# Three moves in a two-layer fp32 kernel: the copies of half 0's y, the next batch's first input products, and the next layer's weight remainders

## The reference

```
x = x + attention(norm(x))        # 16 heads of 128, causal with a position bias
x = x + ternary_ffn(norm(x))      # weights quantized by groups of 64, silu(gate)*up, rms norm
x = x + mamba(norm(x))            # below
x = x + sparse_ffn(norm(x))       # silu(gate)*up, 2 of 4 neighbours kept, down product
```

```
x, z = split(in_proj(h))                      # "input products": 512 channels each
x = silu(causal_conv4(x))
dt_low, B_n, C_n = split(x_proj(x))
delta = softplus(dt_proj(dt_low) + bias)
h_n[t] = exp(delta*A_n)[t] * h_n[t-1] + (delta*B_n*x)[t]     # the scan, over t = 0..1023
y[t] = sum_n h_n[t]*C_n[t] + D*x[t]
out = out_proj(y * silu(z))
```

## Time and profile before

| | us |
|---|---|
| median of 3 runs | 1705.2 |
| the profiled execution | 1710.48 |
| its span, as the profile shows it | 1708.7 |
| PE / DVE / ACT / POOL busy | 1608.9 / 1366.3 / 1231.1 / 789.7 |
| mean granted TensorE clock over the span | 0.982 of full speed |

### The profile page before, as it was taken

How to read it: one execution, slowest core, us unless ns; L and a number is a source line. 1 busy time by engine, 2 the same in 40 slices (tenths; PEclk the granted TensorE clock), 3 DMA queues, 4 the chain that set the end, 5 groups by cost and what they waited for, 6 DMA issues and landing times.

```text
span 1708.7 us, 32910 instructions
## 1 busy us (share of the span) xinstructions
PE 1608.9 (94%) x10396; PEld 1437.8 (84%) x10396; DVE 1366.3 (80%) x2301; ACT 1231.1 (72%) x2307; POOL 789.7 (46%) x753
## 2 busy tenths in 40 slices
PE   8999999999999999999998899878889888889998
PEld 7899889988998899889987788678877687877888
DVE  7788878887887788778876667689985789896997
ACT  5777777777777777777776555599995699994443
POOL 4444444444444444444443111359983199891000
PEclk9999999999999999999999999989999999999999
DMA  3100000000000000000000100013220033240000
GB/s 100 32 20 19 25 31 18 18 25 31 16 16 26 28 16 15 25 28 15 15 7 1 52 0 0 2 72 112 99 100 12 2 112 110 87 158 2 7 19 26
DMA packets 25080, 64.11 MB, mean 38 GB/s; under 512 B 2832, under 2 KB 8976, under 8 KB 24752
## 3 DMA queue, kind: packets, MB, share of 16 engines
q1 hardware_dynamic: 25008, 63.17, 11.0%
HBM read 60.94 MB, written 2.23 MB: 37 GB/s over the span
## 4 chain that ended last, share of the span: by engine, by line
PE 65%; POOL 17%; DVE 8%; issue 6%; ACT 2%; DMA 1%; POOLq 0%; DVEq 0%; SPq 0%; ACTq 0%
POOL m_h L2588 15%; PE ps L579 11%; PE ps L541 11%; PE ps L564 7%; PE ps L496 7%; PE ps L592 5%; PE ps L519 5%; PE ps L814 4%; PE ps L721 4%; PE ps L826 2%; PE ps L742 2%; POOL prob L2452 1%; POOL prob L2445 1%; PE ps L1082 1%; PE ps L506 1%
## 5 line engine op out<-in xcount | busy, mean ns | idle before, releaser
L2452 POOL TENSOR_SCALAR prob<-prob,rinv 128x128 f32<-128x128 f32 (+7 forms) x256 | 228.4, 899 | 212.1 <-DVE rinv L1770 205.7
L2445 POOL TENSOR_SCALAR prob<-prob 128x128 f32<-128x128 f32 (+7 forms) x256 | 188.2, 735 | 288.4 <-ACT prob L1186 279.9
L2588 POOL TENSOR_TENSOR m_h<-m_h,m_C 128x1024 f32<-128x1024 f32 x128 | 300.0, 2375 | 42.2 <-DVE m_h L2353 41.7
L2353 DVE TENSOR_TENSOR_SCAN m_h<-m_y,ps 128x1024 f32<-128x1024 f32 x128 | 287.1, 2276 | 30.6 <-PE ps L970 18.3
L1736 DVE TENSOR_TENSOR pt_lo<-ps,pt_hi 128x512 fp32r<-128x512 f32 (+2 forms) x320 | 189.5, 604 | 81.6 <-ACT pt_hi L1199 79.8
L1729 DVE CUSTOM_DVE_ANT_0 prob<-prob,bias 128x128 f32<-128x128 f32 (+7 forms) x256 | 213.9, 853 | 7.8 <-POOL prob L2445 4.7
L1186 ACT ACTIVATE prob<-ps 128x128 f32<-128x128 f32 (+7 forms) x256 | 165.7, 652 | 68.7 <-PE ps L541 68.1
L1199 ACT ACTIVATE pt_hi<-ps 128x512 fp32r<-128x512 f32 (+2 forms) x320 | 163.0, 531 | 65.9 <-PE ps L564 63.8
L1192 ACT ACTIVATE prob<-prob,nmax 128x128 f32<-128x128 f32 (+7 forms) x256 | 198.1, 776 | 3.0 <-DVE nmax L1729 2.0
L1573 ACT ACTIVATE m_u<-m_uT,m_bT 128x256 f32<-128x256 f32 x448 | 185.6, 504 | 0.1
L978 PE MATMUL ps<-ident,m_h 128*128 128x128 f32 x1024 | 140.4, 281 | 36.8 <-POOL m_h L2588 34.7
(11 more groups left out here) (271 smaller groups left out, 4064.6 us busy)
## 6 DMA issues: line engine op xcount, KB each, us to landing
m_C<-bc_dram SPq DMA_DIRECT2D x64, 512.0 KB, 3.6
wqk_raw<-wqk_in SPq DMA_DIRECT2D x16, 512.0 KB, 3.5
wv_raw<-wv_in SPq DMA_DIRECT2D x16, 256.0 KB, 2.6
wo_raw<-wo_in SPq DMA_DIRECT2D x16, 256.0 KB, 2.8
q_raw<-wgu_in SPq DMA_DIRECT2D x8, 256.0 KB, 2.7
raw<-wgu_in SPq DMA_DIRECT2D x1, 2048.0 KB, 8.3
out<-x SPq DMA_DIRECT2D x8, 256.0 KB, 2.1
x<-x_in SPq DMA_DIRECT2D x2, 512.0 KB, 4.5
```

What stands on the lines that cost most here:

```text
L2353: nc.vector.tensor_tensor_scan(m_h[:, 2 * (v % 2) + e, :], m_da[:, 2 * (v % 2) + e, :], drive(e), 0.0, ALU.mult, ALU.add).then_inc(scan_do ...
L2445: nc.gpsimd.tensor_scalar(prob[:, at:at + n], prob[:, at:at + n], CLIP, -CLIP, ALU.min, ALU.max).then_inc(s_clipped, 1)
L2452: nc.gpsimd.tensor_scalar(prob[:, at:at + n], prob[:, at:at + n], rinv[:, k:k + 1], 1.0, ALU.mult, ALU.mult).then_inc(norm_done, 1)
L2588: nc.gpsimd.tensor_tensor(state, state, m_C[:, v, :], ALU.mult).then_inc(hc_done, 1)
```

## The change

Four places. In the order of the diff: PE's `expand` of unit 12 goes behind `add_state` of unit 9 and `add_x` 8 and 9; the first two input products of the next batch go into the end of the scan, one ahead of each of the two last `add_state` (they wait for the scan of unit 30, which frees banks 4 and 5), with ACT copying them from there as before; ACT's copies of y are split, two behind each decay (units 12 and 13); DVE makes weight remainders 1 and 2 ahead of `dve_sparse_rows_lo`.

```
@@ pe_mamba_scan
             pe.wait_ge(scan_done, unit(b, 1, *at(12)) + 3)
             pe_y_turn(pe, b, 0)
-            expand(1, *at(12), after_y=True)
             add_state(1, *at(9))
             add_x(1, 8)
             add_x(1, 9)
+            expand(1, *at(12), after_y=True)
             pe.wait_ge(scan_done, unit(b, 1, *at(13)) + 3)
             pe_y_turn(pe, b, 1)
             add_state(1, *at(10))
...
             for e in range(2):
+                if b < B - 1:
+                    pe.wait_ge(scan_done, unit(b, 1, last, RING - 1, 0) + 5)
+                    pe_in_x(pe, b + 1, (e,))
                 add_state(1, last, RING - 1, e, end=True)
@@ block.tensor
             pe_mamba_scan(pe, 0)
-            pe.wait_ge(scan_done, 4 + 2 * HALF_UNITS)
-            pe_in_x(pe, 1, range(2))
             pe.wait_ge(yz_done, 3)
             pe_mamba_out(pe, 0, (0, 1), range(4))
@@ act_mamba_scan
-            def decays(half, it, v):
+            def decays(half, it, v, y0=False):
                 for e in range(2):
                     act.wait_ge(scan_done, unit(b, half, it, v, e) + 1)
                     nc.scalar.activation(m_da[:, 2 * (v % 2) + e, :], m_delta[:, 2 * half + e, :], ACT.Exp,
                                          scale=negA[:, bass.ds(it * (RING * DT) + (DT * v + 2 * half + e), 1)]
                                          ).then_inc(da_done, 1)
+                    if y0:
+                        act_y0(act, b, e)
 
             def four(half, it, y0=False):
                 for v in range(RING):
-                    decays(half, it, v)
-                    if y0 and v == 2:
-                        act_y0(act, b)
+                    decays(half, it, v, y0=y0 and v == 2)
                     if v < RING - 1:
                         spread(half, it, v + 1)
@@ act_y0
-        def act_y0(act, b):
-            for e in range(2):
-                for c in range(2):
-                    act.wait_ge(y0_turned, 4 * b + 2 * e + c + 1)
+        def act_y0(act, b, e):
+            for c in range(2):
+                act.wait_ge(y0_turned, 4 * b + 2 * e + c + 1)
...
@@ dve_mamba_end
             dve_ffn_weights(dve, [0])
             dve_sparse_norm(dve, 0)
+            dve_ffn_weights(dve, [1, 2])
             dve_sparse_rows_lo(dve, 0)
-            dve_ffn_weights(dve, [1, 2, 3])
+            dve_ffn_weights(dve, [3])
```

More of the change, by code:

```diff
@@ L1608, in act_mamba_scan, with act_y0 @@
             four(1, last)
[L1610 to L1615, removed]
+        def act_y0(act, b, e):
+            for c in range(2):
+                act.wait_ge(y0_turned, 4 * b + 2 * e + c + 1)
+                nc.scalar.activation(m_yc[:, e, c * BANK:(c + 1) * BANK], ps[:, y_bank(b, e) + c, :],
+                                     ACT.Copy).then_inc(y0_copied, 1)
         def act_y1(act, b, tiles):
```

## The result

| | before | after |
|---|---|---|
| median of the runs, us | 1706.1 (4 runs) | 1692.7 (4 runs, 1691.5 to 1694.4) |
| ratio of times | | 0.9924 (95%: 0.9908 to 0.9940) |
| profiled execution, us | 1710.5 | 1693.6 |
| its span | 1708.7 | 1691.8 |

The account below looks back on a forecast made before the run. The prediction took ACT to pace the scans and PE to lead the chains behind them. Its gains, 2.4 + 3.8 + 4.0 + 4.1 = 14.3 us, taken from 1705.2 gave 1690.9, about 1691, range 1687.5 to 1697.5.

Parts of the forecast that it names:

- ACT paces the scan: In the two scans, ACT needs 4.87 us per state against POOL's 4.65, so only ACT's idle moments lose time.
- Part 1, batch 0, 2.4: At batch 0's y copies in half 1, reordering PE and ACT starts everything behind 2.36 us earlier.
- Part 1, batch 1, 3.8: At batch 1's y copies, the same reordering gains 3.8 us, of which 1.5 is clock.
- the prediction's signs: Trace marks named beforehand; at the y copies, DVE's wait before unit 13 near 0.9 us in both batches.
- Part 2, 4.0: At the end of batch 0's scan, moved input products start the output product 4.0 us earlier; bounds 1.3 and 4.7.
- Part 3, 4.1: Behind batch 1's scan, earlier weight remainders gain 2.3 us of PE waiting and 1.8 of clock; bounds 2.3 and 4.1.
- Nothing late behind them: Behind the changed places, the other engines keep up or move along, so no gain is lost.
- Sum: Whole kernel: 2.4 + 3.8 + 4.0 + 4.1 = 14.3 us gained, giving about 1691; chance 0.63.
- (a): Clock falls at the gaps left at the y copies and the gate, costing 6.4 us: 1697.3; chance 0.19.
- (b): Something unmoved behind the changed places, or busy DVE and ACT, takes part back: 1695; chance 0.11.
- (c): The gate's gap lowers the clock along PE's whole chain behind it, adding 24 us: 1714.8, slower; chance 0.03.
- (d): The change does nothing that counts, as runs without a profile have other waits: 1705; chance 0.04.

Follow-up runs that it names:

- e7: The changed kernel with ACT's seventh scaled copy per state left out, and with it the seventh token tile's input terms; 1690.2 us, ratio to before 0.9902.
- e4: The kernel before with only ACT's order of the y copies changed, two behind each decay; 1704.3 us in one run.
- e5: The kernel before with only PE's order changed, unit 12's expansion behind add_state 9 and two add_x; 1703.2 us in one run.
- e2: The kernel before with only the first two input products of batch 1 moved into the end of batch 0's scan; 1703.4 us, ratio 0.9987.
- e1: The kernel before with only PE's and ACT's order around the y copies changed; 1699.6 us, ratio to before 0.9964.
- e9: The kernel before with 12 filler transposes on PE ahead of each of batch 0's last two add_state; 1701.7 us in one run.

## Why the prediction was right, step by step

- **ACT paces the scan**: right for what the prediction needed: ACT never waits in half 1 but at the copies, and what was taken from that wait came off the half. But its rows were of the last units; over most of half 0 POOL is the one without idle time (e7), and ACT's margin is 0.1 us a unit. The prediction named 4.87 against POOL's 4.65 and did not say how little that leaves to gain.
- **Part 1, batch 0, 2.4**: right in each step: 3.90 and 3.18 from unit to unit (1.04 less before unit 12 and 1.32 before unit 13 had been worked out; 1.08 and 1.32 measured), ACT's idle time 0.25 (0.37), and e4 and e5 show the two terms one by one.
- **Part 1, batch 1, 3.8**: the trace gave 3.84, and DVE waits 0.90 before unit 13, as the prediction's signs had it. But 1.5 of it is clock, which without the change fell there in 2 of 5 traces only.
- **Part 2, 4.0**: the trace gave 4.03, with the chunks where they were put, the last L978 at its 1.09 and the output product 1.32 behind it. What was mis-sized, as a gain of the runs, is the term as such: 4.0 is worth 1.2 where the clock does not fall, and the mean over the 6 traces of unchanged code is 10.2 - 7.4 = 2.8. e2 measured 2.2 in the runs.
- **Part 3, 4.1**: 2.60 + 1.53. The 2.3 was too small by 0.3, as the next instruction starts before the modelled end of the last one (PE's 7.07 us of L1085 overlap the first L814). The 1.8 of clock was 1.53, as 48 products at full clock take 11.2 and not four times 2.75, and it was there to be won in 4 of 6 traces.
- **Nothing late behind them**: right. From the first output product to batch 1's scan 0.45 was lost and in batch 1's half 0 0.37 came back; e2 (72.13 and 77.87) and e1 (72.47 and 77.42) show both pairs, so it is a variation of the stretch and not the change.
- **Sum**: 14.3 with all falls of the clock that the trace of before happened to have; without any of them 2.4 + 2.4 + 1.2 + 2.6 = 8.6; with each at its share of the traces 2.4 + 3.0 + 2.8 + 3.6 = 11.8. The runs gave 13.0 and 14.0 by the ratio, with intervals of 10 to 16 and 11 to 17, so all that can be said is that the sum was about right and on the high side of what the parts alone add up to (6.1 + 2.2 + 2.7 = 11.0). The step that took the waits and the low clock of one trace to be in all runs held for the waits and not for the clock: the trace was of an execution slower than any run, with a fall at all three places. That 1691 came out within 2 us of the median is luck to that extent.
- **Rivals**: (a), that the clock falls at the gaps that are left, did not come: 0 of 7 traces at each of the three places. Its counterargument, that a single gap does nothing, is weaker than it looked, as e1's clock fell behind a gap of 1.44 with the second still to come. The Trainium skill's rule (TensorE: Matmul & The Clock Gate, "A second HAM failure mode: psum-queue depth-cycling"), that frequent short idle times make the clock swing, agrees with the kernel before only in part: gaps of 1.4 to 2.9 were followed by a low clock in some executions and not in others, and the gaps left, 0.4 and 1.3, in none. (b) did not come either: what behind the places could have taken time back moved with them. (c) and (d) are refuted; (c)'s time should read 1714.9.

## What to carry to other kernels

Before pricing a stall, find the engine that never rests in the loop: a stall costs what it makes that engine idle, and its cure pays until the next engine's pace (here 0.1 us a unit away). Split a gain into the part that is order and the part that is clock; one trace shows the clock of one execution, and stretches of unchanged code in other traces say how often it falls. Compare profiles from landmark to landmark: code that nobody touched differed by 5 us between traces, the longer ones at the lower granted clock.

## What the hardware showed that I had not expected

- The same idle times of PE, 1.43 and 1.22, were followed by a window at clock 0.51 in one execution and 1.00 in another. Over identical code the stretch that holds them, from the last scan's start to the output product, took from 8.57 to 11.39 us.
- The first part of the program, up to batch 0's first scan, has the same instructions in all 14 traces and took from 1131.3 to 1136.6 us, at a granted clock of 0.99 in the shortest (e9) and 0.98 in the longest (e4).
- A DVE copy with a scale, 256 columns of fp32, took 0.50 us between scans, 0.42 from its start to the next scan's, where I had taken 0.33 from the four instructions of the norm, which take 1.39 together.
